# The up product of 64 routed experts formed transposed, its turning step removed, and the down product moved one expert forward

## The reference, cut to what matters

```
g = einsum("ech,ehi->eci", buf, w_gate)      # 128 x 256 times 256 x 88
u = einsum("ech,ehi->eci", buf, w_up)        # 128 x 256 times 256 x 88
y = einsum("eci,eih->ech", silu(g) * u, w_down)   # 128 x 88 times 88 x 256
y_tok = y[flat_e, p] * topk_w                # and summed over a token's experts
```

## Time and profile before

| | |
|---|---|
| median of three runs | 425.78 us |
| the profiled execution's own time | 427.13 us |
| its span, first to last instruction | 425.4 us |
| mean granted TensorE clock | 0.953 of full speed |
| expert loop, first turn of rows to last scatter landed | about 64 to 298 us of the span |
| second layer after it | about 299 to 425 us |

### The profile page before, as it was taken

How to read it: one execution, slowest core, us unless ns; L and a number is a source line. 1 busy time by engine, 2 the same in 40 slices (tenths; PEclk the granted TensorE clock), 3 DMA queues, 4 the chain that set the end, 5 groups by cost and what they waited for, 6 DMA issues and landing times.

```text
span 425.4 us, 7089 instructions
## 1 busy us (share of the span) xinstructions
PE 342.8 (81%) x2108; PEld 269.3 (63%) x2108; DVE 298.6 (70%) x950; ACT 208.5 (49%) x536; POOL 252.4 (59%) x237
## 2 busy tenths in 40 slices
PE   0998678997889898989799897695058888988893
PEld 0983345675766676768687776484037777877773
DVE  3699834647778864546467656745569988899875
ACT  3734235434543462474244443422137797776771
POOL 3683025656776756687878878855376556653211
PEclk9999699999899999999899999969659999999998
DMA  7954934457686879887787877535840000000001
GB/s 264 374 180 131 373 99 109 108 108 186 136 189 131 226 173 276 238 195 173 151 187 158 188 179 153 93 45 62 258 138 0 8 20 25 27 25 27 2 25 52
DMA packets 33033, 58.42 MB, mean 137 GB/s; under 512 B 3723, under 2 KB 20451, under 8 KB 32611
## 3 DMA queue, kind: packets, MB, share of 16 engines
q1 hardware_dynamic: 20707, 39.08, 28.1%
q0 software_dynamic: 12288, 18.88, 25.4%
HBM read 40.22 MB, written 17.73 MB: 136 GB/s over the span
## 4 chain that ended last, share of the span: by engine, by line
PE 36%; DVE 22%; DMA 14%; issue 12%; ACT 8%; POOL 7%; SPq 0%; POOLq 0%; DVEq 0%; ACTq 0%
DMA acc_d<-W,idxE 6%; DMA W<-tok_d,idxE 5%; PE two L1515 5%; PE two L1535 4%; PE two L1659 3%; PE two L1400 3%; POOL acc_d L497 3%; PE two L1547 3%; PE two L1475 2%; PE two L1626 2%; PE two L1524 2%; POOL W L478 2%; DMA x<-in_q 2%; DVE F L1262 2%; POOL ny L540 1%
## 5 line engine op out<-in xcount | busy, mean ns | idle before, releaser
L497 POOL DMA_INDIRECT acc_d<-W,idxE x64 | 102.9, 1608 | 47.9 <-DVE W L1083 25.0
L478 POOL DMA_INDIRECT W<-tok_d,idxE x56 | 57.8, 1032 | 40.8 <-DVE idxE L1045 24.0
L1119 DVE SCALAR_TENSOR_TENSOR W<-W,two 128x88 f32<-128x88 f32 x64 | 15.6, 243 | 58.2 <-ACT W L714 58.0
L698 ACT ACTIVATE W<-two 128x256 f32<-128x256 f32 x64 | 24.3, 380 | 39.8 <-PE two L1524 38.6
L1515 PE MATMUL two<-A,v 128*128 128x128 f32 x256 | 36.0, 301 | 7.5 <-issue 6.4
L1515 PEld LDWEIGHTS two<-A,v 128*128 128x128 f32 x256 | 34.7, 214 | 10.2 <-issue 9.6
L1659 PE MATMUL two<-W,A 128*128 128x257 f16 x256 | 30.0, 274 | 10.8 <-DVE F L1287 10.1
L1659 PEld LDWEIGHTS two<-W,A 128*128 128x128 f16 x256 | 23.9, 97 | 16.5 <-DVE F L1287 11.9
L1626 PE MATMUL two<-F,wfcT 128*128 128x256 f16 x256 | 32.0, 280 | 1.4 <-DVE F L1225 1.4
L782 ACT ACTIVATE two<-two,gwv 128x512 f32<-128x512 f32 x32 | 21.4, 667 | 23.3 <-PE two L1626 23.3
L1475 PE MATMUL two<-kT,vT 128*128 128x512 f32 x64 | 30.4, 597 | 2.4 <-DVE F L1036 1.4
(11 more groups left out here) (239 smaller groups left out, 872.5 us busy)
## 6 DMA issues: line engine op xcount, KB each, us to landing
W<-in_gu SPq DMA_DIRECT2D x20, 352.0 KB
acc_d<-F SPq DMA_DIRECT2D x2, 2176.0 KB, 14.2
F<-in_gu SPq DMA_DIRECT2D x12, 352.0 KB
W<-in_dn SPq DMA_DIRECT2D x20, 176.0 KB
tok_d<-xr SPq DMA_DIRECT2D x2, 1280.0 KB, 5.8
F<-in_dn SPq DMA_DIRECT2D x12, 176.0 KB
x<-in_q SPq DMA_DIRECT2D x4, 512.0 KB, 7.1
A<-in_Wo SPq DMA_DIRECT2D x1, 2048.0 KB, 12.6
```

The source lines that it names most:

```text
L478: pool.indirect_dma_start(out=xg[n % XR], out_offset=None, in_=tok_d[:, :], in_offset=bass.IndirectOffsetOnAxis(ap=idxE[:, n:n + 1], axis=0))\
L497: pool.indirect_dma_start(out=acc_d[n % 2][:, :], out_offset=bass.IndirectOffsetOnAxis(ap=idxE[:, n:n + 1], axis=0), in_=ysb[n % YS], in_o ...
L698: sc.activation(xgT[n % 2], bk_(2)[:, 0:D].rearrange("p (k n) -> p k n", k=KH), ACT.Copy)\
```

## The change

The two products of `up(n)` are formed with the expert's weights as the stationary operand (two halves of 88 columns each) and the transposed tokens as the moving one (128 columns). The result in PSUM is 88 x 256: gate transposed in the first 128 columns, up transposed in the next 128. ScalarE's tanh and VectorE's two operations then work on 88 x 128 blocks, and the second of the two writes the transposed hidden block `hT` that the down product takes as its stationary operand. `turn_h`, `take_h` and their semaphores are gone. The down product of expert n-1 (before: n-2) stands right behind `up(n)`, and `put` follows it: `put(n-1)` in step n.

```
-        eth = [W[:, 6656 + 128 * r:6656 + 128 * r + FF] for r in range(2)]
-        h = [W[:, 6912 + 128 * r:6912 + 128 * r + FF] for r in range(2)]
-        gu = [bk_(6 + r)[:, 0:2 * FF] for r in range(2)]
-        hT_bank = [bk_(6 + r)[0:FF, 256:256 + CAP] for r in range(2)]
+        ethT = [W[0:FF, 6656 + 128 * r:6784 + 128 * r] for r in range(2)]
+        guT = [bk_(6 + r)[0:FF, 0:2 * CAP] for r in range(2)]
...  ScalarE
-            def take_h(n):
-                sc.wait_ge(hT_ps, n + 1)
-                if n >= 2:
-                    sc.wait_ge(y_ps, n - 1)
-                sc.activation(hT[n % 2], hT_bank[n % 2], ACT.Copy).then_inc(hT_ready, 1)
...
-                    sc.wait_ge(h_ready, n - 1)
-                sc.activation(eth[n % 2], gu[n % 2][:, 0:FF], ACT.Tanh, scale=0.5).then_inc(gtanh_ready, 1)
-                if n:
-                    take_h(n - 1)
+                    sc.wait_ge(hT_ready, n - 1)
+                sc.activation(ethT[n % 2], guT[n % 2][:, 0:CAP], ACT.Tanh, scale=0.5).then_inc(gtanh_ready, 1)
...  VectorE
-                    ve.wait_ge(hT_ps, n - 1)
-                then(ve.scalar_tensor_tensor(out=h[n % 2], in0=eth[n % 2], scalar=1.0, in1=gu[n % 2][:, 0:FF],
+                    ve.wait_ge(y_ps, n - 1)
+                then(ve.scalar_tensor_tensor(out=hT[n % 2], in0=ethT[n % 2], scalar=1.0, in1=guT[n % 2][:, 0:CAP],
                                              op0=ALU.add, op1=ALU.mult))
-                ve.tensor_tensor(h[n % 2], h[n % 2], gu[n % 2][:, FF:2 * FF], ALU.mult).then_inc(h_ready, 1)
-                if n >= 2:
-                    put(n - 2)
+                ve.tensor_tensor(hT[n % 2], hT[n % 2], guT[n % 2][:, CAP:2 * CAP], ALU.mult).then_inc(hT_ready, 1)
+                if n:
+                    put(n - 1)
...  TensorE
-                for k in range(KH):
-                    ins = pe.matmul(gu[n % 2], xgT[n % 2][:, k, :],
-                                    wgu[r][:, n % WG, k, :], start=(k == 0), stop=(k == KH - 1))
+                for m in range(2):
+                    for k in range(KH):
+                        ins = pe.matmul(guT[n % 2][:, CAP * m:CAP * m + CAP], wgu[r][:, n % WG, k, FF * m:FF * m + FF],
+                                        xgT[n % 2][:, k, :], start=(k == 0), stop=(k == KH - 1))
-            def turn_h(n):
-                pe.wait_ge(h_ready, n + 1)
-                pe.transpose(hT_bank[n % 2], h[n % 2], ident[:, :]).then_inc(hT_ps, 1)
...
-                if n >= 1:
-                    turn_h(n - 1)
                 if n == SUM_AT:
                     pe.wait_ge(gsum_ready, 2)
-                    pe.wait_ge(y_ready, n - 2)
+                    pe.wait_ge(y_ready, n - 1)
...
-                if n >= 2:
-                    down(n - 2)
+                if n:
+                    down(n - 1)
...  after the loop
-            turn_h(NE - 1)
-            for n in range(NE - 2, NE):
-                down(n)
+            down(NE - 1)
```

More of the change, by code:

```diff
@@ L286, in build @@
         xg_ld = [sem(f"xg_ld{r}") for r in range(XR)]
-        xgT_ps, xgT_ready, gu_ps, gtanh_ready, h_ready, hT_ps, hT_ready, y_ps, y_ready = [sem(n) for n in (
-            "xgT_ps", "xgT_ready", "gu_ps", "gtanh_ready", "h_ready", "hT_ps", "hT_ready", "y_ps", "y_ready")]
+        xgT_ps, xgT_ready, gu_ps, gtanh_ready, hT_ready, y_ps, y_ready = [sem(n) for n in (
+            "xgT_ps", "xgT_ready", "gu_ps", "gtanh_ready", "hT_ready", "y_ps", "y_ready")]
         y_added = [sem(f"y_added{i}") for i in range(2)]
@@ L743, in _ @@
                     sc.activation(wpoT[:, :, :], wpoT[:, :, :], ACT.Copy, scale=0.5).then_inc(wpo_ready, 1)
-            take_h(NE - 1)
             sc.activation(warm[:, :], warm[:, :], ACT.Gelu)
@@ L1145, in _ @@
                     low_weights()
-            for n in range(NE - 2, NE):
-                put(n)
+            put(NE - 1)
             def centre_weights():
```

## The result

The changed kernel is slower, by a little: 426.57 us (median of 20 runs, one odd run of 907.12 us among them left out of the comparison) against 425.00 us; ratio 1.0053, 95% interval 1.0033 to 1.0072. I had forecast -0.2 us; it is +1.6 us here. Run again beside the experiments, each time on another chip, the same kernel gave three further ratios to the kernel before: 1.0012 (0.9985 to 1.0039), which is no difference that can be told, 1.0026 (1.0001 to 1.0051), and, in six runs, 1.0132 (1.0085 to 1.018).

The account below looks back on a forecast made before the run. GpSimd was taken to pace mid-loop, TensorE and VectorE before 136 us and after 262.68 us. -0.4 + 1.5 + 0.7 - 1.44 - 0.52 = -0.2 us: 426.9 us profiled, 425.6 us median; range 420 to 431.5.

Parts of the forecast that it names:

- TensorE, VectorE and ScalarE per expert: Each expert: TensorE +0.19 us at 0.112 us a pass, VectorE +0.11 us, ScalarE loses a 0.265 us copy.
- First stretch: Loop up to 136 us: put 16 comes 3.36 us earlier against 2.96 us of added work, so GpSimd starts 0.4 us earlier.
- bound of +2.9 us: Slower limit for the loop up to 136 us, if weight loads set the pace of the up product's passes.
- Second stretch: Loop to 262.68 us: TensorE's extra 3.4 us covered by 4.1 us of gather waits; waits for landed scatters add 1.5 us.
- +1.5 us, VectorE stands for landed scatters: Mid-loop to 262.68 us: earlier puts wait for the scatter four experts back, delaying the attention product by 1.5 us.
- My example: Put 55, moved one expert earlier, waits 2.5 us on VectorE for scatter 51, issued at 259.42, landing at 264.3.
- The first rival: Mid-loop: the four output slots hold up VectorE and TensorE loses its room; 431.1 us, chance 0.16.
- Third stretch: From 262.68 us to the last scatter: +0.7 us up to the last attention product, then -1.44 and -0.52 us.
- +0.7: Before the last attention product: VectorE +0.11, two up products +0.19 each, about 0.2 waiting for put 61.
- The second rival: Up product in every expert: weight loads pace it at 0.157 us a pass, +0.55 us an expert; 434.8 us, chance 0.06.
- the third: Rival for the whole loop: early idle time hides the longer product, GpSimd keeps a 3.4 us lead; 421.6 us, chance 0.16.
- The range: Whole kernel time: 420 to 431.5 us, with the first rival and half of the third included.

Follow-up runs that it names:

- b_tail_early: Kernel before, with the last two experts' turn, down products and puts moved ahead of the last PV (attention product) step: 424.69 us, ratio 0.9979.
- b_again: The kernel before, unedited, run and profiled a second time: 426.01 us, ratio 1.0022.
- a_third: The changed kernel, unedited, run again on another chip: 425.98 us, ratio 1.0012 to the kernel before.
- a_fourth: The changed kernel, unedited, run again beside the kernels with TensorE time added or removed: 426.14 us, ratio 1.0026 to the kernel before.
- a_ys5: The changed kernel with five slots for scaled outputs instead of four: 426.29 us, ratio 1.0001 to the kernel before.
- a_again: The changed kernel, unedited, run and profiled again, six runs: 430.54 us, ratio 1.0132 to the kernel before.
- set 1: First four follow-up kernels on one chip: both kernels unedited, before with 0.22 us more TensorE per expert, changed with 0.22 us less; 426.01, 430.54, 427.79, 427.68 us.
- sets 1 and 2: First eight follow-up kernels, each set of four on its own chip; the second set varied order, tail, slots and weight sums of the changed kernel: 427.7 to 431.47 us.
- sets 3 and 4: Last eight follow-up kernels, each set of four on its own chip: repeats, slots, tail, moved weight sums, TensorE time added or removed; 422.69 to 434.47 us.
- a_plus2: The changed kernel with one more two-pass matmul per up product, 0.22 us more TensorE per expert: 434.47 us, ratio 1.0224 to the kernel before.
- a_minus2_b: Repeat of a_minus2 in a later set, 0.22 us less TensorE per expert than the changed kernel: 422.69 us, ratio 0.993 to the kernel before.
- a_minus2: The changed kernel with one of four up-product matmuls left out, 0.22 us less TensorE per expert: 427.68 us, ratio 1.007 to the kernel before.
- b_plus2: The kernel before with one more two-pass matmul per up product, 0.22 us more TensorE per expert: 427.79 us, ratio 1.0056.

## Why the prediction was wrong

In short: the forecast let the longer up product cost nothing in mid-loop. It used up all of TensorE's waits for gathers and still made the loop up to turn 58 longer, by 1.2 to 5.0 us depending on the execution of before; against that the shorter tail gave 2.0.

**TensorE, VectorE and ScalarE per expert: right.** 0.11 us a pass, 0.28 us where I had 0.30 for a VectorE operation, 0.27 us for the tanh.

**First stretch, "GpSimd's even run starts 0.4 us earlier": right for GpSimd, and read for the wrong engine.** Scatter 16 was 1.1 us earlier: put 16 came at 134.23 us and its scatter at 135.28, before them 135.65 and 136.41. But TensorE itself was 2.4 us later at turn 20 (74.1 against 71.7, with one half-clock stretch of 3.4 us in each): most of its added time had not been hidden, only the puts had been moved ahead of it. I had the 2.3 us in my own working and then dropped it, since the stretch was judged by GpSimd's start. (The bound of +2.9 us of this stretch should read +3.2: 12 x 0.55 - 3.36.)

**Second stretch, "18 x 0.19 = 3.4 us more from 204 us on, and has 4.1: covered": this is the step that failed.** The bill must be drawn up from the first expert. By turn 58 the change adds 58 x 0.19 = 11.0 us to TensorE, and what it had to give were its waits for gathers, 7.1 us in the profile that I read, of which I took those behind 204 us against the need behind 204 us. The changed kernel is later at turn 58 by 199.9 less 198.7, 196.8 and 194.9, which is 1.2, 3.1 and 5.0 us; together with the waits that were used up, 7.1, 5.4 and 4.0, that is 8.3, 8.5 and 9.0 us. The stretch from turn 0 to turn 58 shows the rest of the account (columns as in the earlier trace rows: before, b_tail_early, b_again, the changed kernel):

```profile
63.99:262.68 198.69, 176.70 (x1026) 138.29 (x1025) 127.17 (x400) 90.63 (x277) 142.46 (x111) 0.98 0.74 173
63.60:260.42 196.82, 174.37 (x1026) 136.81 (x1026) 126.27 (x399) 89.75 (x276) 142.76 (x110) 0.99 0.73 174
63.91:258.84 194.93, 175.04 (x1026) 137.80 (x1026) 127.33 (x401) 90.48 (x277) 141.85 (x110) 0.98 0.75 177
63.50:263.38 199.88, 184.02 (x1200) 149.99 (x1200) 130.23 (x399) 82.02 (x220) 150.48 (x113) 0.98 0.75 174
```

TensorE's idle time is 22.0, 22.5, 19.9 and 15.9 us. Without the waits for gathers it is 14.9, 17.0, 15.9 and 15.9: against b_again nothing but the gathers gave way, against b_tail_early 1.1 us of other idle time did as well, and against before the other idle time grew by 1.0. Its busy time, less half of the half-clock stretches (3.4, 1.7, 3.4 and 3.4 us), rose by 7.3, 8.0 and 9.0 us, and not by 11.0. So 0.19 us per expert was too much as well, by a fifth to a third, though the spacing of the passes was right; where that difference lies, no run separates. TensorE's waits for gathers in the profile of before, then in b_again (total, times, longest):

```profile
PE two L1524 <- DMA W<-tok_d,idxE: 7.1, 8, 1.5
```

```profile
PE two L1524 <- DMA W<-tok_d,idxE: 4.0, 4, 1.3
```

The same program, and 4.0 us apart in time. I had also read the room off one execution, and it was the one with the most of it: where the gathers come late, TensorE has more room and the whole takes longer. Then I took the difference found there over to the median of all runs. b_tail_early's 5.4 us is near the middle.

**"+1.5 us, VectorE stands for landed scatters": wrong.** The puts waited 0.3 us in the first profile and not at all in a_third and a_fourth, and a_ys5 removes the cause for nothing. My example set put 55 at 261.84 us against scatter 51 at 259.42. In the first profile they stand 7.2 us apart (timelines of GpSimd and VectorE):

```profile
256.31 1.59 POOL L495 DMA_INDIRECT acc_d<-W,idxE  x1 [0.30 <-issue]
```

```profile
263.54 0.47 DVE L1072 TENSOR_SCALAR W<-two,F 128x256 f32<-128x256 f32 x1
```

The scatter is 3.1 us earlier than I had left it, and the put, behind a late TensorE, 1.7 us later: the landing is past. The mechanism exists (10.1 and 6.3 us when TensorE is faster by 0.22 us an expert), one step beyond the kernel that I predicted. Against the profile that I read, this charge stood in by luck for the debt that I had put at nothing: the attention product that I had moved from 264.10 to 265.6 us began at 264.91. The first rival falls with it: TensorE lost its room, but not for the slots.

**Third stretch:** -1.96 as forecast. From turn 58 to last PV I had +0.7; it was 26.3 us against 26.5 before and 26.4 in b_again. What hid it is, in part, the clock behind the two reduces: half speed from 276.4 to 283.3 before, half of that after (same columns).

```profile
276.40:283.30 6.90, 4.70 (x25) 4.48 (x26) 3.64 (x11) 0.50 (x2) 3.10 (x2) 0.75 0.43 45
```

With the long stretch (6.8 us) and the same product, a_ys5 takes 26.8 us and a_again 27.0, which is 0.3 to 0.6 us above before. The rest of the 0.7 did not come.

**Sum as it should have been:** +3.1 at turn 58 against the middle profile of before, and -2.1 from there to scatter 63 (29.6 us against 31.8 before and 31.7 in b_again), is +1.0 us. The three sets without a wait of ScalarE gave +1.6, +0.6 and +0.6 by medians (+2.3, +0.5 and +1.1 by ratios). The second rival fell with the spacing of 0.11; of the third (a lead of 3.4 us that is kept) 1.1 us came at scatter 16, and nothing behind it. The range held the time.

**What the sum doesn't cover: +5.3 us in set 1.** There a_again's ScalarE stood at the first shared copy, and in the first profile it did not (timelines of ScalarE, a_again, then the changed kernel's first):

```profile
71.58 0.60 ACT L658 ACTIVATE xr<-two 128x512 f32<-128x512 f32 x1 [3.89 <-remote]
73.75 0.59 ACT L653 ACTIVATE A<-two 88x512 f32<-88x512 f32 x1 [1.57 <-remote]
```

```profile
68.88 0.60 ACT L658 ACTIVATE xr<-two 128x512 f32<-128x512 f32 x1 [1.20 <-PE two L1398]
```

TensorE's product for the copy (timeline: 1.03 us from 67.76 and from 67.81 us) had ended at 68.8 us in both. In the profiles of sets 1 and 2 all seven edited or changed kernels show such a wait (1.9 to 4.0 us at L658 or its like), b_again none; in sets 3 and 4 no profile does, a_third, a_fourth, a_plus2 and a_minus2_b among them. a_minus2 and a_minus2_b are one kernel, 1.4% apart with and without it. So the wait goes with the chip or the set, and there with the edited programs, and a_again's later turn 40 (144.4) with it, beside 3.8 us of put waits. What ScalarE waits for I have not shown ("remote" names no engine of the core). A 16 KB instruction packet is moved at 68.2 to 68.3 us in these two traces, with and without the wait, and at 76.3 us in b_plus2, well behind a like wait that ended at 70.2. So there, at least, that packet isn't the cause. It stays open.

## What to carry to other kernels

When an edit lengthens the work of one engine in a long loop, add up its whole debt from the first iteration and its whole idle time, rather than the balance of the stretch you look at; arrears do not lapse where another engine's queue hides them. Read the room from more than one execution, because here the execution that waited most for gathers was also the longest of the three. And price the dose beyond the edit: the kernel before took 0.22 us more per expert for 1.4 to 2.4 us, and the changed kernel another 0.22 us for 8.3.

## What was unexpected of the hardware

TensorE's clock was granted more evenly when it had more to do. The changed kernel has three half-clock stretches of 3.4 us in the loop; the last follows 4.37 us in which TensorE stood for a put behind the reduces (timeline of TensorE, then the stretch, columns as in the earlier trace rows). Before has a like wait of 4.23 us there.

```profile
278.60 0.74 PE L1532 MATMUL two<-F,W 88*128 88x256 f32 x2 [4.37 <-DVE W L1072]
```

```profile
279.10:282.50 3.40, 3.40 (x17) 3.38 (x17) 1.04 (x5) 0.00 (x0) 2.73 (x2) 0.50 0.33 39
```

a_plus2, 8 us longer, has only this last one, and a mean clock of 0.966 against 0.958 in the changed kernel and 0.946 in a_minus2_b (TensorE busy 358.8, 348.7 and 340.5 us). A single profile is thin evidence, since one kernel's clock varies by 0.01 between executions; but the medians over all runs go the same way, 0.962, 0.950 to 0.956 in its four sets, and 0.946. Up to turn 58 half clock cost 0, 3.4 and 5.1 us. So a part of what is saved on TensorE is given back in clock, and a part of what is added is repaid.
